# Expert tile rows fetched in four feature groups and turned in 32x32 blocks on VectorE

## What is computed

```python
logits = jnp.einsum('bsd,de->bse', x, gate_w) + gate_b
probs = jax.nn.softmax(logits, axis=1)
vals, idx = jax.lax.top_k(probs, K)                     # K = 2
h = jax.nn.relu(jnp.einsum('bsd,edo->ebso', x, w1) + b1[:, None, None, :])
h = jax.nn.relu(jnp.einsum('ebso,eop->ebsp', h, w2) + b2[:, None, None, :])
y = jax.nn.relu(jnp.einsum('ebso,eop->ebsp', h, w3) + b3[:, None, None, :])
...
v = jnp.einsum('ebso,bse->eo', y, w_tok)
out = jnp.einsum('bse,eo->bso', ind, v)
```

## Time and profile before

| | us |
|---|---|
| median of three runs | 1004.35 (1003.84, 1004.35, 1006.84) |
| span of the profiled execution | 1003.7 |
| median less that span | 0.65 |
| stage of the 60 units, first layer-0 product to last product | 439.3 to 669 |
| PE busy | 934.0 (93%) |
| DVE, ACT, POOL busy | 429.3, 346.5, 250.9 |
| DMA queue of SP | 70048 packets, 156.54 MB, 45.8% of 16 engines |

### The profile page before, as it was taken

The page is one execution under the profiler, slowest core; times in us unless marked ns, Lnnn a source line. Parts: engine busy times, 40 slices in busy tenths (PEclk is TensorE's granted clock), DMA queues, the critical chain, the costliest instruction groups (busy, mean ns, idle before and its releaser), DMA issues. The chain is left out here.

```text
span 1003.7 us, 19227 instructions
## 1 busy us (share of the span) xinstructions
PE 934.0 (93%) x7747; PEld 757.2 (75%) x7747; DVE 429.3 (43%) x994; ACT 346.5 (35%) x886; POOL 250.9 (25%) x306
## 2 busy tenths in 40 slices
PE   5999999989998889999999999999889899999994
PEld 5977776676775644789999999987765578999532
DVE  2973454224442647002112132135267630656576
ACT  2322323245552124122222233324276611122374
POOL 5452111023554306000000010004065403000275
PEclk9999999999999979899999999997969998999996
DMA  9994000245622807259999888700040032971001
GB/s 254 382 331 127 2 2 2 98 152 203 238 120 95 309 7 254 55 181 386 358 383 313 284 269 283 254 29 28 4 153 3 2 119 78 321 247 66 1 15 51
DMA packets 72456, 162.01 MB, mean 161 GB/s; under 512 B 4132, under 2 KB 5685, under 8 KB 70321
## 3 DMA queue, kind: packets, MB, share of 16 engines
q1 hardware_dynamic: 70048, 156.54, 45.8%
q0 software_dynamic: 2320, 4.25, 1.4%
HBM read 128.81 MB, written 31.97 MB: 160 GB/s over the span
## 5 line engine op out<-in xcount | busy, mean ns | idle before, releaser
L2113 PE MATMUL ps<-ffn_h,ffn_w 128*128 128x128 f32 x1280 | 149.1, 275 | 0.0
L2113 PEld LDWEIGHTS ps<-ffn_h,ffn_w 128*128 128x128 f32 x1280 | 145.9, 192 | 0.0
L2113 PE MATMUL ps<-ffn_xh,ffn_w 128*128 128x128 f32 x640 | 74.9, 275 | 0.3 <-ACT ffn_xh L2147 0.3
L2203 DVE TENSOR_SCALAR ffn_h<-ps,tile_bias 128x128 f32<-128x128 f32 x80 | 22.5, 345 | 122.4 <-PE ps L2113 122.4
L2113 PEld LDWEIGHTS ps<-ffn_xh,ffn_w 128*128 128x128 f32 x640 | 73.1, 192 | 0.9 <-issue 0.9
L1418 POOL TENSOR_TENSOR ctx_low<-shelf,ctx_high 128x1024 fp32r<-128x1024 f32 (+2 forms) x24 | 43.0, 1819 | 65.4 <-PE ps L1283 33.7
L2161 ACT ACTIVATE ffn_y<-ffn_y 128x128 f32<-128x128 f32 x80 | 23.7, 298 | 73.9 <-DVE ffn_y L2219 73.9
L1526 PE MATMUL ps<-x_qT,ctx_ct 128*128 128x100 f32 (+1 forms) x384 | 46.4, 284 | 2.3 <-PEq L137 2.0
L1526 PEld LDWEIGHTS ps<-x_qT,ctx_ct 128*128 128x128 f32 (+1 forms) x384 | 45.0, 197 | 3.7 <-issue 3.2
L2219 DVE SCALAR_TENSOR_TENSOR ffn_y<-ps,tile_bias,ffn_gate_row 128x128 f32<-128x128 f32 x80 | 22.6, 344 | 58.0 <-PE ps L2113 57.9
L2834 POOL TENSOR_TENSOR att_e<-att_e,decay 100x400 f32<-100x400 f32 x32 | 32.7, 1033 | 46.1 <-DVE att_e L2685 46.1
(11 more groups left out here) (469 smaller groups left out, 2096.8 us busy)
## 6 DMA issues: line engine op xcount, KB each, us to landing
ffn_w<-in_L_ffn_w_dram SPq DMA_DIRECT2D x60, 1024.0 KB, 6.0
shelf<-in_ctx_dram SPq DMA_DIRECT2D x12, 1280.0 KB
expert_rows<-nothing SPq DMA_DIRECT2D x1, 14820.0 KB, 49.6
context_turned<-ctx_ct SPq DMA_DIRECT2D x8, 1444.0 KB, 7.9
ctx_ct<-context_turned SPq DMA_DIRECT2D x8, 1444.0 KB, 12.5
ctx_lent<-in_ctx_dram SPq DMA_DIRECT2D x4, 1280.0 KB
rows_own<-expert_rows SPq DMA_DIRECT2D x8, 260.0 KB, 3.0
x_wo<-in_L_xattn_Wo_dram SPq DMA_DIRECT2D x1, 2048.0 KB, 9.5
```

The source lines that it names most:

```text
L2113: mm = nc.tensor.matmul(acc(n)[:, m, :], w[:, n % SLOTS, k, m * P:(m + 1) * P], into[l][:, i % 2, k, :], start=k == 0, stop=k == C - 1, sk ...
L2203: nc.vector.tensor_scalar(h2[:, i % 2, m, :], acc(n)[:, m, :], bsel[:, m, i, 1:2], 0.0, ALU.add, ALU.max).then_inc(h2_kept, 1)
```

## The change

A tile's rows are read in four DMAs of 32 rows each, in which partition f*32 + r takes 128 features (512 bytes) of row r, the f-th quarter; the gates come in a fifth DMA with a semaphore of its own. DVE then turns the tile in 32x32 blocks with one instruction of 128x512 into `ffn_xh`, whose free dimensions become (row group, k, row in the group). Chunk k of the product now holds the features f*128 + k*32 + d on partition f*32 + d. The first-layer weights are put in the same order: four DMAs, one for each k, each of 128 rows of 2 KB taken as 4 groups of 32. The transposes on PE and the copies on ACT go away. The gathers of tiles 6 to 19 follow every second load, from that of unit 5 to that of unit 31, and the six loads of later weights those of units 32 to 37.

```diff
+        first_w = g["L0_ffn_w1"].rearrange("e (f k d) o -> f d e k o", f=HPC, k=C)
+        expert_w = [g[f"L0_ffn_w{i}"].rearrange("e (c p) o -> p e c o", p=P) for i in (2, 3)]
...
+        parts_of = lambda n: C if units[n][1] == 0 else 1
+        landed_by = [16 * sum(parts_of(m) for m in range(n % SLOTS, n + 1, SLOTS)) for n in range(len(units))]
...
-            sp.dma_start(w[:, n % SLOTS, :, :], expert_w[l][:, bass.ds(expert, 1)].rearrange("p a c o -> p (a c) o")
-                         ).then_inc(w_landed[n % SLOTS], 16)
+            if l == 0:
+                for k in range(C):
+                    sp.dma_start(w[:, n % SLOTS, k, :], first_w[:, :, bass.ds(expert, 1), k, :].rearrange("f d a o -> f d (a o)")
+                                 ).then_inc(w_landed[n % SLOTS], 16)
+            else:
+                sp.dma_start(w[:, n % SLOTS, :, :], expert_w[l - 1][:, bass.ds(expert, 1)].rearrange("p a c o -> p (a c) o")
+                             ).then_inc(w_landed[n % SLOTS], 16)
...
-            sp.dma_start(rows_of_tile(i), rows_dram[bass.ds(row, P), :]).then_inc(gathered[i], 16)
+            here = rows_dram[bass.ds(row, P), :]
+            for n in range(HPC):
+                sp.dma_start(rows_of_tile(i)[:, n * P:(n + 1) * P],
+                             here[n * HD:(n + 1) * HD, 0:D].rearrange("r (f d) -> f r d", d=P)).then_inc(gathered[i], 16)
+            sp.dma_start(rows_of_tile(i)[:, D:XW], here[:, D:XW]).then_inc(gathered_gates[i], 16)
...
+        xh = sb("ffn_xh", [P, 2, HPC, C, HD], F32, ff)
...
-                    if n >= SLOTS - 1 and more < MT:
-                        gather(sp, more)
-                        more += 1
+                    if n >= SLOTS - 1 and more < MT:
+                        if n % 2:
+                            gather(sp, more)
+                            more += 1
...
-                def turn(i):
-                    pe.wait_ge(gathered[i], 16)
-                    if i >= 2:
-                        pe.wait_ge(kept, i - 1)
-                    for c in range(C):
-                        mm = nc.tensor.transpose(ps[:, 3 + i % 2, c * P:(c + 1) * P], rows_of_tile(i)[:, c * P:(c + 1) * P],
-                                                 ident[:, :])
-                    mm.then_inc(turned, 1)
...
+                            rhs = xh[:, i % 2, :, k, :] if l == 0 else into[l][:, i % 2, k, :]
...
-                def keep(i):
-                    act.wait_ge(turned, i + 1)
-                    if i >= 2:
-                        unit_made(act, i - 2, 0)
-                    nc.scalar.activation(xh[:, i % 2, :, :], ps[:, 3 + i % 2, :].rearrange("p (c t) -> p c t", c=C),
-                                         ACT.Identity).then_inc(kept, 1)
...
+                def turn(i):
+
+                    dve.wait_ge(gathered[i], 16 * HPC)
+                    if i >= 2:
+                        unit_made(dve, i - 2, 0)
+                    nc.vector.transpose(xh[:, i % 2].rearrange("p i k r -> p (i k r)"), rows_of_tile(i)[:, 0:D]).then_inc(kept, 1)
```

More of the change, by code:

```diff
@@ L1777, in program @@
         fold_bank = lambda n: ps[:, (7, 0, 1)[n % 3], :]
-        gathered = [sem(f"rows_gathered{i}") for i in range(MT)]
+        gathered, gathered_gates = ([sem(f"{what}_gathered{i}") for i in range(MT)] for what in ("rows", "gates"))
         def gather(sp, i):
             row = sp.value_load(table[0:1, 1, i:i + 1], min_val=0, max_val=SPARE)
-            sp.dma_start(rows_of_tile(i), rows_dram[bass.ds(row, P), :]).then_inc(gathered[i], 16)
+            here = rows_dram[bass.ds(row, P), :]
[3 more added lines that the diff above has]
+            sp.dma_start(rows_of_tile(i)[:, D:XW], here[:, D:XW]).then_inc(gathered_gates[i], 16)
         with nc.Block() as block:
@@ L2016, in program @@
         RING = 3
-        xh, h1, h2 = (sb("ffn_" + n, [P, 2, C, P], F32, ff) for n in ("xh", "h1", "h2"))
+        xh = sb("ffn_xh", [P, 2, HPC, C, HD], F32, ff)
+        h1, h2 = (sb("ffn_" + n, [P, 2, C, P], F32, ff) for n in ("h1", "h2"))
         into = (xh, h1, h2)
@@ L2022, in program @@
         vT = sb("ffn_vT", [P, C, MT], F32, ff)
-        turned, kept, made, h1_kept, h2_kept, gated, gate_col, gate_rows, rows_kept, weighed, counted, v_flip, v_hi, v_lo, by_tile, tile_kept = (
-            sem("ffn_" + s) for s in ("turned", "kept", "made", "h1_kept", "h2_kept", "gated", "gate_col", "gate_rows",
+        kept, made, h1_kept, h2_kept, gated, gate_col, gate_rows, rows_kept, weighed, counted, v_flip, v_hi, v_lo, by_tile, tile_kept = (
+            sem("ffn_" + s) for s in ("kept", "made", "h1_kept", "h2_kept", "gated", "gate_col", "gate_rows",
                                       "rows_kept", "weighed", "counted", "v_flip", "v_hi", "v_lo", "by_tile", "tile_kept"))
@@ L2064, in _ @@
                 for s in range(SLOTS):
-                    sp.wait_ge(w_landed[s], 16 * (len(units) // SLOTS))
+                    sp.wait_ge(w_landed[s], landed_by[len(units) - SLOTS + s])
             @block.tensor
             def _(pe):
-                def turn(i):
-                    pe.wait_ge(gathered[i], 16)
-                    if i >= 2:
-                        pe.wait_ge(kept, i - 1)
-                    for c in range(C):
-                        mm = nc.tensor.transpose(ps[:, 3 + i % 2, c * P:(c + 1) * P], rows_of_tile(i)[:, c * P:(c + 1) * P],
-                                                 ident[:, :])
-                    mm.then_inc(turned, 1)
                 def spread_gate(i):
@@ L2103, in layer @@
                     i, l = units[n]
-                    pe.wait_ge(w_landed[n % SLOTS], 16 * (n // SLOTS + 1))
+                    pe.wait_ge(w_landed[n % SLOTS], landed_by[n])
                     if n >= RING:
@@ L2112, in layer @@
                                 pe.wait_ge((h1_kept, h2_kept)[l - 1], C * i + k + 1)
+                            rhs = xh[:, i % 2, :, k, :] if l == 0 else into[l][:, i % 2, k, :]
                             mm = nc.tensor.matmul(acc(n)[:, m, :], w[:, n % SLOTS, k, m * P:(m + 1) * P],
-                                                  into[l][:, i % 2, k, :], start=k == 0, stop=k == C - 1,
+                                                  rhs, start=k == 0, stop=k == C - 1,
                                                   skip_group_check=True)
                     mm.then_inc(made, 1)
-                turn(0)
                 for n, (i, l) in enumerate(units):
-                    if n + 1 < len(units) and units[n + 1][1] == 0:
-                        turn(units[n + 1][0])
                     if l == 1:
@@ L2162, in total @@
                                              accum_out=vT[:, m, i:i + 1]).then_inc(counted, 1)
-                keep(0)
                 for n, (i, l) in enumerate(units):
-                    if n + 1 < len(units) and units[n + 1][1] == 0:
-                        keep(units[n + 1][0])
                     if 0 <= n - PREP_AT - 1 < len(PREP):
@@ L2220, in weigh @@
                                                        ALU.add, ALU.mult).then_inc(weighed, 1)
+                turn(0)
                 for n, (i, l) in enumerate(units):
+                    if n + 1 < len(units) and units[n + 1][1] == 0:
+                        turn(units[n + 1][0])
                     if l == 0:
@@ L2243, in _ @@
                 for i in range(MT):
-                    pool.wait_ge(gathered[i], 16)
+                    pool.wait_ge(gathered_gates[i], 16)
                     if i >= 2:
```

1 line of the change is left out of this document (removed).

## The result

| | before | after |
|---|---|---|
| median, us (runs, range) | 1004.1 (4, 1003.7 to 1006.84) | 1191.69 (4, 1189.76 to 1194.56) |
| ratio, 95% interval | | 1.1865 [1.1838, 1.1893] |
| span of the profiled execution | 1003.7 | 1192.8 (its own time 1194.56) |
| mean granted clock of the span | 0.957 | 0.897 |

What follows compares the result with a forecast made beforehand. The prediction took PE as the bound before and four DMA engines after: 407.9 us from 419.4 put unit 54 at 829, 183 us late; 1003.7 + 183 + 3.6 = 1190 span, so 1191 us, range 1125 to 1262.

Steps and rivals of the forecast that it cites:

- PE side, 8.5 us: Stage of the 60 units: turns leaving PE save 7.9 us between units and 0.6 at the start, if DMAs keep pace.
- Four engines, set by the DRAM side's 4: Row and first-layer weight pieces: a leading 4 gives always the same four of 16 engines; chance 0.84.
- Packets of 512 B, 44 ns: Gathers in pieces: 128 packets at 44 ns on each of four engines, 5.6 us a gather, 112.6 for 20.
- The pieces' packets, 84 ns: First-layer weight pieces: 128 packets of 2 KB at 84 ns per engine, 10.75 us a load, 193.5 for 18.
- Ordinary loads, 2.7 us each: The other 34 loads among units 3 to 54, still on 16 engines: 2.7 us each, 91.4 in all.
- The sum, 407.9 us: Work of the busiest four engines from the first gather at 419.4 us; unit 54 lands at 829, 183 us later.
- the sign: Whole kernel: slower with chance 0.88, faster by over 0.3% with 0.10, within 0.3% with 0.02.
- Start of the stage: Gather issues before the barrier at 437.8 us: it comes some us late, but that is inside the 407.9 us.
- Clock, 3.6 us: Last six units: after idling PE runs at the lower clock, one unit counted twice, 3.6 us (0 to 10.7).
- Rival A: Pieces spread over all 16 engines, DMA work stays hidden, the full 8.5 us come back: 995.8 us; chance 0.11.
- Rival B: Only the rows suffer, the weights spread; unit 31 lands at 612 instead of starting at 558: 1054 us; chance 0.03.
- Rival C: The change works, but reading runs of 32 or issue work (18 us for 24 issues) eats 8.5 us: 1004; chance 0.02.

Runs made afterwards that it cites:

- turn_only: The kernel before with the turn on DVE alone, gathers and first-layer weights loaded as before; 997.79 us against 1007.22, ratio 0.9917.
- both_by_quarter: The changed kernel with rows and first-layer weights cut into one DMA per group of 32 partitions, DRAM side leading with 32; 1051.58 us, ratio 1.0461.
- sixteen_groups: The changed kernel with rows cut by groups of 32 partitions and first-layer weights as 16 groups of 8 rows; 1037.6 us in one run.
- four_whole_pieces: sixteen_groups with the four weight DMAs each led by 128 plain rows on both sides; 1005.62 us in one run beside 1005.55.
- weights_by_quarter: The changed kernel with only the first-layer weights cut by groups of 32 partitions, rows still in pieces leading with 4; 1071.71 us in one run.
- quarters_two_in_flight: both_by_quarter with one more wait on SP, load n issued only when load n-2 has landed; 1033.12 us in one run.

## Why the prediction was right

- **PE side, 8.5 us.** Right: turn_only gained 0.83%, with 0.70 us a turn and nothing for runs of 32. In the changed kernel it does not show, as forecast.
- **Four engines, set by the DRAM side's 4.** Right, by the shares of 0.25, by four small packets a piece, and by the doses of 4, 8, 16 and 128 with the SBUF side at 128 throughout. This was the choice on which all rested, taken at 0.84. The rule of the Trainium skill quoted there ("DMA: Bandwidth & Descriptors", "Why a DMA increments its semaphore by 16 and not by 1") agrees in both cases that no row of before held: unequal counts on the two sides, and a leading 8.
- **Packets of 512 B, 44 ns.** Too high. From 425 to 440 us, gathers alone:

```profile
DMA packets 2410, 0.94 MB, mean 63 GB/s; under 512 B 596, under 2 KB 2410, under 8 KB 2410
...
q1 hardware_dynamic: 2410, 0.94, 24.4%
```

 1814 packets of 512 B took at most 0.244 x 240 = 58.6 us, 32 ns each. The factor of 1.37 for rows 2080 B apart, taken over from whole rows, did not apply. Twenty gathers: at most 82 us in place of 112.6.
- **The pieces' packets, 84 ns.** Nearly right: at most 89 alone.
- **Ordinary loads, 2.7 us each.** Too low. A late tile takes 833.77 - 814.40 = 19.4 us against 16.2 (10.75 + 2 x 2.7), and 10.75 of them are the pieces. That leaves 4.3 us for each ordinary load; over the whole stage (next point) it is 3.7. Its packets took 136 ns while they ran on all 16 engines, where before had 87. I had assumed that engines shared with pieces would serve ordinary loads as before, and had read the 87 as a fixed price: the trace of before itself has 104 ns from 540 to 570 us, 3.3 us a load.
- **The sum, 407.9 us.** Measured 411.4, from the first gather's issue at 422.36 to unit 54 at 833.77. With rows at 82, pieces at 193.5 and the later weights at 10.4, (411.4 - 285.9)/34 = 3.7 us are left for an ordinary load (3.3 if the pieces' packets cost 89 ns). So two mis-sized terms cancel: 31 us less of rows, 34 x 1.0 = 34 us more of loads. That the forecast met within 1 us is partly luck; the sign, and a loss between 140 and 240 us, are not.
- **Start of the stage.** The issues cost 0.7 us a piece with its gap, so that the barrier fell at 448.1, "some us late" as said. The first gather itself was issued 2.9 us later than in the earlier trace rows, because PE's work ahead of it ran longer at the lower clock: from 370 to 375 us the granted clock was 0.50, where before had 0.92. turn_only, which has no pieces, shows 0.50 too, and both_by_quarter, with as many DMAs, 0.94; so it is not the change, and why is not explained.
- **Clock, 3.6 us.** Too high by 1.3: the last idle stretch cost 5.95 - 3.65 = 2.3 us at unit 54.
- **Rival A, 995.8.** Its arithmetic was wrong even for its own case: both_by_quarter and sixteen_groups do have 16 engines and came to 1051.6 and 1037.6. I priced their packets at the 87 ns of plain loads. Had the pieces spread in either of these ways, the kernel would still have been slower than before; even the plain pieces of four_whole_pieces gave 1005.6. The sign had less to fear than 0.11.
- **Rival B, 1054.** weights_by_quarter is its nearest relation, 1071.7, with the dear packets inside.
- **Rival C.** As a cause of the loss it is refuted, by turn_only for the turn and the operand and by four_whole_pieces for the number of DMAs. But its price of the issue work was right: with pieces on 16 engines the first six gathers of four_whole_pieces take from 422.19 to 440.48 us, 18.3 where it had 18, and that kernel ends at 1005.6, near its 1004. PE also misses 4.2 us from 510 to 600 us there, so the issue work is not shown to be what eats the gain.

```profile
422.19 1.87 SPq L1792 DMA_DIRECT2D rows_own<-expert_rows  x4
...
440.13 0.35 SPq L1794 DMA_DIRECT2D rows_own<-expert_rows  x1
```

## What to carry to other kernels

Before a DMA is cut or reordered, read the leading count of its DRAM side: 4 gives four engines of 16, and a stage whose DMA share is near 1 then stretches by what those four must carry. A full DMA share is no proof of full speed either: compare the GB/s at equal share. Beside the same rows by quarter, loads that are not dealt as plain 128-partition ones moved 257 to 274 GB/s at 1.09 while PE waited; plain ones moved 307 at 1.05, all that PE asked for, and before had 378 at 1.03. Work saved on the engine that is the bound is kept only if what feeds it doesn't grow.

## What the runs showed that was not expected

- A packet of 2 KB costs 87 to 104 ns in plain loads on 16 engines, at most 89 with only four engines at work, and about 140 on 16 engines when the rows are dealt in 16 or 32 leading steps. Ordinary loads that share the stage with four-engine pieces also rise to 136. Why is open: the ports are one candidate, two loads side by side another (quarters_two_in_flight, with the extra wait, gained 18 us in its one run).
- An issue on SP, with its gap, takes 0.45 us for a DMA on 16 engines (1.81 us for four) and 0.72 on four (2.87), and up to 5.8 us for one piece late in the stage. What is queued behind it waits: from 794 to 800 us the share is 0.27 and the next ordinary load is issued only at 801.6.
- DVE turns 128x512 float32 in 32x32 blocks in 0.70 us, no dearer than its copy, but in 1.10 us when it reads with a step of 4.
